# Two tiles, batches or channel blocks per operation, and a new order of calls, in a two-layer gated transformer kernel

## What is computed

```python
x = x + tanh(g_xattn[0]) * wkv_scan(w, u, k=layernorm(x), v=context)     # recurrence over the 256 tokens of a batch
x = x + tanh(g_ffn[0])   * ffn(layernorm(x), ternary weights, tokens rounded to integers)   # 256 -> 1024 -> 256
x = x + tanh(g_xattn[1]) * attention(layernorm(x), context)              # 32 heads of 8, q and k RMS-normed
x = x + tanh(g_ffn[1])   * (top-8 of 64 experts + a shared expert)(layernorm(x))            # experts 256 -> 64 -> 256
```

## Time and profile before

| | |
|---|---|
| median of 3 runs | 495.06 us (493.48 to 495.15) |
| the profiled execution | 494.8 us, of which the span from first to last instruction is 493.0 us |
| busy: PE, DVE, ACT | 402.1, 384.8, 306.3 us |
| instructions: PE, DVE, ACT | 2612, 871, 476 |
| granted PE clock, mean | 0.947 of full |

### The profile page before, as it was taken

One profiled execution on the slowest core, in us unless ns is written; L12 is line 12 of the kernel. 1 busy time (PEld: TensorE's weight loads), 2 busy tenths in 40 slices (PEclk: granted clock), 3 DMA queues, 4 the chain that ended last, 5 costly groups with the idle time before them and its releaser, 6 DMA issues.

```text
span 493.0 us, 7922 instructions
## 1 busy us (share of the span) xinstructions
PE 402.1 (82%) x2612; PEld 192.2 (39%) x2612; DVE 384.8 (78%) x871; ACT 306.3 (62%) x476; POOL 0.2 (0%) x4
## 2 busy tenths in 40 slices
PE   1041757686775899989999898999999999999996
PEld 1020244331423445544334433444444444444443
DVE  5999488999998789999877867887446777766754
ACT  5889585689894695558888657555333444455422
POOL 0000000000000000000000000000000000000000
PEclk9996799595998699999999999999999999999999
DMA  8520000000020151525336241333420655555511
GB/s 299 203 64 1 0 1 1 1 0 2 2 65 1 43 172 54 161 59 169 95 110 192 69 136 64 108 107 117 127 73 26 213 180 169 176 162 161 182 42 43
DMA packets 31507, 47.47 MB, mean 96 GB/s; under 512 B 5610, under 2 KB 15210, under 8 KB 30956
## 3 DMA queue, kind: packets, MB, share of 16 engines
q1 hardware_dynamic: 31468, 46.98, 30.2%
HBM read 45.65 MB, written 1.31 MB: 95 GB/s over the span
## 4 chain that ended last, share of the span: by engine, by line
PE 47%; DVE 31%; ACT 7%; issue 7%; DMA 5%; SPq 2%; DVEq 0%; ACTq 0%
PE ps L1608 25%; PE ps L1941 12%; PE ps L1713 4%; DMA regP<-in_dp_dram 4%; DVE tiny L1215 2%; PE ps L1701 2%; DVE regW L1298 2%; DVE bn L1030 2%; ACT regO L594 1%; DVE xn L1049 1%; DMA regC<-in_ctxT_dram 1%; DVE regF L1227 1%; DVE rep L1176 1%; PE ps L1629 1%; DVE regW L1518 1%
## 5 line engine op out<-in xcount | busy, mean ns | idle before, releaser
L1608 PE MATMUL ps<-hH,regC 128*128 128x512 f16 x264 | 85.5, 379 | 1.3 <-ACT regW L949 1.1
L1518 DVE TENSOR_TENSOR regW<-ps,regW 128x512 f32<-128x512 f32 x64 | 44.2, 690 | 50.4 <-PE ps L1608 47.9
L949 ACT ACTIVATE regW<-ps 128x512 f32<-128x512 f32 x51 | 30.4, 596 | 83.7 <-PE ps L1608 80.6
L1608 PE MATMUL ps<-hH,regW 128*128 128x512 f16 x248 | 81.8, 386 | 0.7 <-DVE regW L1518 0.6
L1608 PE MATMUL ps<-hL,regC 128*128 128x512 f16 x132 | 50.0, 379 | 0.0
L1941 PE MATMUL ps<-regW,regC 128*128 128x512 f16 x198 | 48.1, 379 | 0.6 <-DVE regW L1501 0.6
L1608 PE MATMUL ps<-hL,regW 128*128 128x512 f16 x124 | 47.8, 385 | 0.0
L1501 DVE TENSOR_TENSOR regW<-regW 128x512 f16<-128x512 f32 x64 | 43.7, 682 | 0.4 <-ACT regW L962 0.3
L1941 PE MATMUL ps<-regW 128*128 128x512 f16 x180 | 43.8, 380 | 0.2 <-DVE regW L1501 0.2
L962 ACT CAST regW<-regW 128x512 f16<-128x512 f32 x64 | 39.2, 612 | 4.4 <-DVE regW L1539 3.9
L1608 PEld LDWEIGHTS ps<-hH,regC 128*128 128x128 f16 x264 | 25.8, 98 | 33.5 <-issue 2.6
(11 more groups left out here) (202 smaller groups left out, 663.4 us busy)
## 6 DMA issues: line engine op xcount, KB each, us to landing
regW<-routing_dram SPq DMA_DIRECT2D x130, 128.0 KB, 3.1
regP<-in_gu_dram SPq DMA_DIRECT2D x56, 256.0 KB, 2.7
regP<-in_dp_dram SPq DMA_DIRECT2D x56, 128.0 KB, 2.8
regO<-in_ffn_dram SPq DMA_DIRECT2D x3, 1024.0 KB, 9.3
x<-in_x_dram SPq DMA_DIRECT2D x2, 512.0 KB, 8.3
regC<-in_ctxT_dram SPq DMA_DIRECT2D x1, 1024.0 KB, 5.3
regP<-in_proj_dram SPq DMA_DIRECT2D x1, 768.0 KB, 12.1
out_dram<-x SPq DMA_DIRECT2D x1, 512.0 KB, 3.5
```

What stands on the lines that cost most here:

```text
L949: nc.scalar.activation(sgm[:, c % 2, :], bank(gate_bank(c)), ACT.Silu, scale=UNSCALE).then_inc(esilu_done, 1)
L1518: V.tensor_tensor(rows, bank(gate_bank(c) + 1), rows, ALU.mult).then_inc(et_done, 1)
L1608: mm = T.matmul(out_ap, w(k), a(k), start=(n == 0), stop=(n == 3 * DK - 1))
```

## The change

What was done per tile, per channel block or per batch is done for two of them in one instruction:

- scan of half 1: c = 2 is both channel blocks. The scans of the sums run through both batches in one instruction of 512 (half 0 too); the states `Pn` and `Qn` lose their batch axis.
- `project(r)`, `row_sums(r)`, `rows_end(r)`: two tiles per call. `high_halves`, `low_halves` and the transposes before them: both channel blocks, in one bank.
- `add_y`, `heads_out` and `experts_residual`: `x` of two tiles in one addition.
- the number of PE instructions and their shapes stay as they are.

All lists and all three tables are written anew. Between chunk 0 and chunk 27 the tables hold the same work but for `turn_rows(8)` and `(9)` with `turned_rows(8)` and `(9)`, which now stand before chunk 0.

```diff
         BESIDE_VECTOR = {
...
-            (14, "C"): [("weights_low", 17), ("weights_low", 18)],
+            (14, "C"): [("split_low", 14), ("split_low", 15), ("weights_low", 16), ("weights_low", 17),
+                ("heads_sum", 21, 6), ("heads_sum", 22, 4)],
...
+            (18, "C"): [("weights_low", 21), ("weights_low", 22)],
...
             def sums_a(c):
-                s, k, v, W, Z = chunk(c)
+                blocks, both, W, v = block_rows(c)
                 dve.wait_ge(exp_done, 4 * c + 2)
                 post(V.tensor_tensor(W["EV"], W["E2"], v, ALU.mult))
-                for b in range(2):
-                    post(V.tensor_tensor_scan(Z["Qn"][:, b, 1:S + 1], W["A2"][:, b, :], W["E2"][:, b, :], 0.0, ALU.mult, ALU.add))
+                for s in blocks:
+                    post(V.tensor_tensor_scan(Qn[:, s, 1:CH + 1], wk["A2"][:, s, :], wk["E2"][:, s, :], 0.0, ALU.mult, ALU.add))
                 settle()
...
-                V.scalar_tensor_tensor(YN[:, s, :], wk["EV"][:, s, :], -2.0, wk["GAP"][:, s, :],
-                                       ALU.add, ALU.mult).then_inc(y_ready, 1)
+                V.scalar_tensor_tensor(YN[:, both, :], W["EV"], -2.0, W["GAP"], ALU.add, ALU.mult).then_inc(y_ready, 1)
...
+            def project(r, b):
+                j, t = 2 * (r % 2), run_tile(r)
+                src = bank(b, 2 if of_keys(r) else 1).rearrange("p (i n) -> p i n", i=2)
+                act.wait_ge(proj_done, r + 1)
...
+                post(nc.scalar.activation(kc[:, j:j + 2, :], src[:, :, 0:D], ACT.Copy, scale=UNSCALE))
...
             def low_halves(q, b0):
                 a, b = NORM_TILES[q]
-                for k in range(DK):
-                    dve.wait_ge(hH_ready, halves_before(q) + k + 1)
-                    V.tensor_tensor(hL[:, k, a * P:b * P], bank(b0 + k)[:, 0:(b - a) * P], hH[:, k, a * P:b * P],
-                                    ALU.subtract).then_inc(hL_ready, 1)
+                dve.wait_ge(hH_ready, splits_before(q) + 1)
+                V.tensor_tensor(hL[:, :, a * P:b * P], bank(b0).rearrange("p (k t) -> p k t", k=DK), hH[:, :, a * P:b * P],
+                                ALU.subtract).then_inc(hL_ready, 1)
...
             def add_y(h, b0):
-                for j in range(HT):
+                for j in range(0, HT, 2):
                     t = h * HT + j
-                    dve.wait_ge(y_turned, (t | 1) + 1)
-                    V.scalar_tensor_tensor(x[:, t, :], bank(b0 + j // 2)[:, (j % 2) * D:(j % 2 + 1) * D], ntg[:, 0:1],
-                                           x[:, t, :], ALU.mult, ALU.add).then_inc(x1_done, 1)
+                    two = x[:, t:t + 2, :].rearrange("p i d -> p (i d)")
+                    dve.wait_ge(y_turned, t + 2)
+                    V.scalar_tensor_tensor(two, bank(b0 + j // 2), ntg[:, 0:1], two, ALU.mult, ALU.add).then_inc(x1_done, 1)
...
             turn_norm(0, 4)
-            project(0, 7)
-            project(1, 6)
             sum_weights()
             turn_y(0, 4)
             turn_norm(1, 6)
-            up_product(0, 4)
+            project(0, 4)
             gate_product(0, 6)
```

More of the change, by code:

```diff
@@ new lines, in bass_flamingo @@
+            (3, "A"): [("weights_low", 6)],
+            (3, "C"): [("weights_low", 7), ("ffn_residual", 5, 7), ("stats", 8), ("norm", 8),
+                ("wide_inner", 7, 0, 5)],
+            (4, "B"): [("low_halves", 8, 7)],
+            (4, "C"): [("ffn_residual", 6, 6), ("weights_low", 8), ("wide_inner", 7, 1, 5)],
+            (5, "C"): [("row_sums", 5), ("rows", 5), ("weights_low", 9)],
+            (6, "C"): [("ffn_residual", 7, 7), ("split_low", 10), ("split_low", 11), ("stats", 9)],
@@ new lines, in bass_flamingo @@
+            (7, "C"): [("norm", 9), ("weights_low", 10)],
+            (8, "C"): [("weights_low", 11), ("row_sums", 6)],
+            (9, "C"): [("rows", 6)],
+            (10, "A"): [("weights_low", 12)],
+            (11, "C"): [("split_low", 12), ("low_halves", 9, 7), ("heads_sum", 16, 6), ("split_low", 13),
+                ("weights_low", 13)],
+            (12, "C"): [("weights_low", 14), ("heads_sum", 17, 7), ("heads_sum", 18, 6), ("weights_low", 15)],
+            (13, "C"): [("row_sums", 7), ("rows", 7), ("heads_sum", 19, 5), ("heads_sum", 20, 4)],
@@ L1089, in sums_a @@
                 settle()
             def sums_b(c):
-                s, k, v, W, Z = chunk(c)
-                for b in range(2):
-                    post(V.tensor_tensor_scan(Z["Pn"][:, b, 1:S + 1], W["A2"][:, b, :], W["EV"][:, b, :], 0.0, ALU.mult, ALU.add))
+                blocks, both, W, v = block_rows(c)
+                for s in blocks:
+                    post(V.tensor_tensor_scan(Pn[:, s, 1:CH + 1], wk["A2"][:, s, :], wk["EV"][:, s, :], 0.0, ALU.mult, ALU.add))
                 settle()
@@ L1363, in _ @@
+            ffn_residual(1, 0)
             stats(2)
             rows_begin(0)
+            ffn_residual(2, 7)
             norm(2)
+            stats(3)
+            low_halves(2, 7)
             rows_end(0)
-            ffn_residual(2, 1)
-            low_halves(2, 6)
-            ffn_residual(3, 3)
+            norm(3)
+            row_sums(1)
+            rows_begin(1)
             split_low(0)
             split_low(1)
-            stats(3)
+            rows_end(1)
+            turned_rows(0, 7)
@@ L1373, in _ @@
+            turned_rows(1, 1)
             row_sums(2)
[L1374 to L1380 removed]
             split_low(2)
             split_low(3)
[L1383 to L1390 removed]
@@ L1441, in _ @@
-            rows(4)
-            heads_sum(14, 2)
-            heads_sum(15, 3)
-            low_halves(5, 6)
-            split_low(8)
-            heads_out(2, 2)
-            split_low(9)
-            heads_out(3, 6)
-            stats(7)
+            heads_sum(8, 7)
+            heads_sum(9, 6)
+            heads_sum(10, 0)
+            norm(6)
+            token_scales(1)
+            rows(4)
+            low_halves(5, 1)
+            heads_sum(11, 7)
+            heads_sum(12, 6)
+            heads_sum(13, 0)
```

894 lines of the change are left out of this document (426 added, 468 removed).

## The result

| | before | the change |
|---|---|---|
| median | 494.72 us (493.48 to 495.15, 4 runs) | 479.91 us (478.72 to 482.10, 4 runs) |
| ratio | | 0.9702, 95% interval 0.9672 to 0.9731 |
| span of the profiled execution | 493.0 us | 478.6 us |
| first expert product | 163.68 us | 157.90 us |
| busy: PE, DVE, ACT | 402.1, 384.8, 306.3 us | 399.1, 379.5, 302.0 us |

The forecast was 487.8 us with a range from 482 to 494.5.

What follows compares the result with a forecast made beforehand. The prediction took DVE's list to set the time from 68.4 us until chunk 0 and PE to bound the kernel after it. Terms -0.6 - 5.4 - 0.9 - 0.1 = -7.0 us took 494.8 to 487.8 us, range 482 to 494.5.

Steps and rivals of the forecast that it cites:

- term A: Until 68.4 us: DVE work leaves the chain to the scan's output, part given back; -0.6 us, between -2.3 and +1.5.
- term B: 68.4 us to chunk 0: merges -2.2, a moved split -0.9, fewer DVE waits -2.3; -5.4 us, between -3.1 and -8.1.
- Chunks 0 to 27: PE taken as the bound: DVE's merges given nothing, PE's idle of 9.1 us left; only -0.9 us forecast.
- term C: Chunks 0 to 27: turn_rows(8) and (9) gone from between the chunks; -0.9 us.
- signs of being wrong: Chunk 0 starting later than 161 us, or PE standing idle 12 us or more after it.
- The rival that PE's idle goes as well: New table spreads DVE's lump in chunk 22 over 22 to 25; half of 9.1 us idle goes, 483.3 us; chance 0.15.
- The rival that PE starves at the weights: Six paired splits in the tables make ACT late and PE wait, 2 us each; 12 us, 499.8 us; chance 0.10.
- The rival of coarser handovers: Wide operations wait for their last producer; five handovers on DVE's path give back 4.5 us, 492.3 us; chance 0.15.

Runs made afterwards that it cites:

- e14: The changed kernel with low_part(1), (2) and high_projections back at their places of before: ratio 0.9751 to the kernel before, first ffn_inner at 57.53 us.
- e16: The changed kernel, order and handovers untouched, with every widened DVE and ACT instruction issued as two of the old width: ratio 0.9797 to the kernel before.
- e13: The change run again, the same kernel: ratio 0.9702 to the kernel before, chunk 0 at 155.19 us.
- e1: The changed kernel with the three tables of the kernel before: 486.4 us, ratio 0.9841 to the kernel before.
- e6: The changed kernel with weights_high(6) on ACT moved behind ffn_turned(5) in chunk 2: 477.5 us, ratio 0.9644 to the kernel before.
- e2: The kernel before with merged operations only, old order throughout: ratio 1.0149 to the kernel before, 6.6 us slower.
- e17: The changed kernel with ACT's splits of weights 28 and 29 paired in chunk 22, 30 and 31 in chunk 25, as before: ratio 0.9787 to before.
- e18: The changed kernel with statistics and norm 11 on DVE back in chunk 22, behind the two heads_out: ratio 0.9791 to the kernel before.
- e20: The changed kernel with old table rows for chunks 22 to 27, but DVE's statistics and norm 11 moved from chunk 22 to 23: ratio 0.9877 to before.

## Why the prediction was off, step by step

- **Until 68.4 us, term A.** Forecast -0.6, measured -0.9 (`ffn_inner` 55.44 for 56.30). `norm(1)` started at 42.23 us, as counted (near 42.2), and the transposes of `turn_y` took 1.94 us. The projection also kept PE at work before the gate products, as hoped: the first of these start 0.216 us apart, where before they started 0.427 us apart, the pace of the lower clock, until 54.9 us. The granted clock of the first window does not tell this by itself: it says 1.00 in the change, though the first three projection products there start 0.43 us apart too. The single profiles scatter by more than the size of the term (54.9 to 56.6 us), so its size is not shown; the 2.0 us of e14 is the better evidence.
- **To chunk 0, term B.** Forecast 157.7 us, measured 157.90 and 155.19. At like clock (0.83 and 0.82) the stretch from the first `ffn_inner` went from 107.4 to 102.5 us, 4.9 for a forecast of 5.4. Right in sum; that chunk 0 came within 0.2 us of the forecast in the first profile is luck, with a scatter of 3.7. Merging was a little under-sized (0.08 us an instruction of DVE's time), and its whole effect in e16, 4.7 us, is larger than DVE's time ahead of chunk 0. The estimate from the fixed latency of the Trainium skill (VectorE: DVE Perf Modes, The TRN2 errata), 156 ns an instruction, was 5.0 us; of the time that an instruction occupies DVE, the 80 ns of the runs are half of that. The waits of DVE should have been under 2 us with one on the exponentials; they were 3.4 us in the first profile and 1.6 in e13, of which 0.2 on the exponentials. The two largest of the first:

```profile
DVE regO L1243 <- PE ps L1702: 0.9, 3, 0.5
DVE hL L1178 <- ACT hH L661: 0.8, 1, 0.8
```

- **Chunks 0 to 27, the step that failed.** "PE is the bound, so I give them nothing. PE's idle, 9.1 us, I leave as it is." Measured, the stretch from chunk 0 to 33 went from 195.1 to 186.6 us (188.2 in e13), where 0.9 was forecast. By e1 (193.3 us) 5 to 7 us of it are the order of the tables. The windows split the 8.6 us: PE's idle time fell by 3.9 (9.1 to 5.2), and its busy time by 4.7 (170.23 to 165.49), although its instructions are the same but for 16 transposes. Of the 4.7, 0.9 is the price that term C gave to these 16, now ahead of chunk 0, and 1.1 the clock, by an estimate: behind the start of chunk 0 PE works at half of it for 4.1 us before and 1.9 in the change, and loses half of the difference (e13 has 4.9 and gains nothing by it). The other 2.7 fit short gaps, which I have not measured one by one: a 128x512 product lasts 0.38 us in the trace and the next starts 0.216 after it, so a stall of up to 0.16 us behind it counts as busy. I took busy 170.23 of 179.3 for a bound of 9.1 us on what could be had, and it was none: e6 has 183.6 us from chunk 0 to 33, 11.6 less than before.
- **The signs of being wrong** that the prediction named, chunk 0 later than 161 us or 12 us of idle time of PE behind it, did not come. On the side on which it failed it had only one of the figures that it expected, "some 9 us" of idle time between chunk 0 and 28, which was 5.2.
- **The rival that PE's idle goes as well** was the right mechanism, with 0.15 of the chance. Its half of the idle time, 4.5 us, is near the 3.9 that went; what it lacked is that the busy time falls too. The evidence lay in rows that I quoted for something else: ACT's 18.3 us before loads and the loads on the chain between 262 and 345 us. I called PE "hardly hurt" by them.
- **The rival that PE starves at the weights** counted the pairs of `weights_low` on DVE. The pairs that matter in these runs are ACT's, since the silu stands behind them. The change has one of these in chunk 2, which cost PE a wait of 3.3 us as described, and breaks up those of chunks 22 and 25.
- **The rival of coarser handovers** is real in the old order, 6.6 us in e2, more than the 4.5 forecast. By the Trainium skill (Perfetto Trace Analysis, Matmuls) independent groups should rotate through banks so that reading overlaps the next; e2 is in line with it, with 12.4 us of waits for 4.0, but no run tells how many of them are for banks. In the new order the waits ahead of chunk 0 are 3.4 and 1.6 us, and there a cost of the rule isn't seen.

## What to carry to other kernels

Merging operations and laying the order anew are one change: tested apart, each can look worthless or harmful. An engine that is busy 95 % of a stretch need not be its bound; read which engine the chain runs on in that stretch, and what it does in the slices where the chain leaves the busy engine. Where loads go into two buffers, look at two consumers of loads in one place of an in-order list: here the second stood 4.7, 2.9 and 4.6 us before its load, and what was behind it in that list was late.

## What the runs showed that I had not expected

The granted clock ahead of chunk 0 differs from one execution of the same kernel to the next and moves a milestone by 2.7 us, while the time of the kernel moves by about 1 us. A wait of PE can cost more than its length: in e13, e17, e18 and e20 the clock was at its lower level for 3.4 us behind it. Keeping PE at work through a gap kept the clock at its upper level until the next wait, 5 us later, and the stretch at half the clock came there. The stretch from chunk 22 to 33 was the same to 0.02 us in the profiles of eight kernels (48.50 to 48.52) and 0.5 us longer in two (49.04 and 49.05), with one wait of 0.45 us more on a probability; one of the two is e13, the same kernel as the change.
